# V loads issued ahead of the two stores of finished tiles, on one queue

## The reference, cut to what matters

```python
x = x + einsum('bct,bcd->bdt', x, w0[subject])        # mixes the 32 rows of a sequence
x = x + einsum('bct,bcd->bdt', x, w1[condition])
x = x + attention(x, ...)                             # below
x = x + (x @ W.T + scale * (x @ A.T) @ B.T)           # one of 8 adapters for 16 batch rows

# attention: q, k, v projected from x, rms norm and rope on q and k
k_blocks[blk, :, off] = k ; v_blocks[blk, :, off] = v # new keys and values go into the paged cache
scores = q . k_all * scale, masked to a window of 128 positions
o = softmax(scores) @ v_all ; return o @ Wo.T
```

## Time and profile before

| | |
|---|---|
| Runs | 490.85, 495.17, 505.08 us |
| Profiled execution | 493.59 us, span of the instructions 491.8 us |
| Busy share of the span | PE 78%, VectorE 70%, ScalarE 54%, GpSimd 22% |
| Mean DMA | 150 GB/s; SyncE's queue 33.5% and GpSimd's 24.9% of 16 engines' span |
| Granted TensorE clock, mean | 0.906 |
| Issue to landing, median | V write-out not told, V load 11.7 us, V rest load 8.8 us, store 7.1 us |

### The profile page before, as it was taken

The page is one execution under the profiler, slowest core; times in us unless marked ns, Lnnn a source line. Parts: engine busy times, 40 slices in busy tenths (PEclk is TensorE's granted clock), DMA queues, the critical chain, the costliest instruction groups (busy, mean ns, idle before and its releaser), DMA issues.

```text
span 491.8 us, 16903 instructions
## 1 busy us (share of the span) xinstructions
PE 381.8 (78%) x6190; PEld 283.1 (58%) x6190; DVE 345.4 (70%) x1017; ACT 264.4 (54%) x977; POOL 107.7 (22%) x178
## 2 busy tenths in 40 slices
PE   1753788888885027888798899999699999899996
PEld 0333534444442025676676777777577777777785
DVE  6995189999999515747666777777567677777782
ACT  3303556666664015646465766676456666766662
POOL 5300043333334700221112112111211212111000
PEclk9855789999998555989989999999989999999999
DMA  3999123222202266888887777967977666976200
GB/s 111 354 409 412 49 69 107 73 79 72 78 35 81 61 140 175 150 188 178 172 183 180 155 177 167 145 156 160 204 192 160 159 175 149 181 182 147 73 23 24
DMA packets 68867, 73.58 MB, mean 150 GB/s; under 512 B 18190, under 2 KB 65326, under 8 KB 66528
## 3 DMA queue, kind: packets, MB, share of 16 engines
q1 hardware_dynamic: 61968, 39.38, 33.5%
q0 software_dynamic: 6864, 33.72, 24.9%
HBM read 70.83 MB, written 26.21 MB: 197 GB/s over the span
## 4 chain that ended last, share of the span: by engine, by line
PE 48%; DMA 19%; ACT 12%; issue 11%; DVE 7%; SPq 1%; DVEq 1%; ACTq 0%; POOL 0%; POOLq 0%
ACT rope L610 6%; PE probT_bank L1128 6%; DMA kvbuf<-new_scratch,winidx 6%; PE out_bank L1152 5%; PE score_banks L1015 5%; PE score_banks L1089 5%; PE probT_bank L1015 4%; DMA value_scratch<-kvbuf 4%; PE keys_bank L1071 3%; PE score_banks L1084 3%; ACT window L601 3%; PE score_banks L1006 3%; DMA window<-value_scratch 3%; PE out_bank L1139 3%; DMA out<-early 3%
## 5 line engine op out<-in xcount | busy, mean ns | idle before, releaser
L610 ACT ACTIVATE rope<-score_banks,negm 128x176 f32<-128x176 f32 x256 | 101.8, 413 | 4.5 <-DVE negm L890 4.5
L890 DVE TENSOR_REDUCE negm<-score_banks 128x2 f32<-128x352 f32 x128 | 61.1, 519 | 34.6 <-PE score_banks L1089 34.1
L900 DVE TENSOR_SCALAR rope<-rope,rinv 128x176 f32<-128x176 f32 x256 | 70.9, 319 | 4.6
L626 ACT COPY early<-probT_bank 128x128 f32<-128x128 f32 x64 | 17.0, 266 | 88.6 <-PE probT_bank L1128 88.6
L433 POOL DMA_INDIRECT new_scratch<-stage,rowidx x32 | 36.5, 1139 | 106.7 <-DVE stage L759 101.7
L907 DVE COPY rope<-probT_bank 128x512 f32<-128x512 f32 x64 | 44.3, 692 | 18.0 <-PE probT_bank L1108 14.3
L610 ACT ACTIVATION_READ_ACCUMULATOR rope<-score_banks,negm 128x1 f32 x256 | 54.2, 212 | 0.0
L1128 PE MATMUL probT_bank<-rope,window 128*32 128x64 f32 x2048 | 43.7, 226 | 5.5 <-issue 4.7
L601 ACT COPY window<-keys_bank 128x352 f32<-128x352 f32 x60 | 46.8, 780 | 1.5 <-PE keys_bank L1071 1.5
L1071 PE MATMUL keys_bank<-ident,kvbuf 88*128 88x88 f32 x240 | 32.5, 260 | 16.3 <-ACT window L601 14.3
L1128 PEld LDWEIGHTS probT_bank<-rope,window 128*32 128x32 f32 x2048 | 32.8, 112 | 17.7 <-issue 17.7
(11 more groups left out here) (184 smaller groups left out, 734.6 us busy)
## 6 DMA issues: line engine op xcount, KB each, us to landing
value_scratch<-kvbuf SPq DMA_DIRECT2D x16, 704.0 KB
window<-value_scratch SPq DMA_DIRECT2D x16, 512.0 KB, 11.7
work<-in_x SPq DMA_DIRECT2D x16, 256.0 KB, 2.7
new_scratch<-window SPq DMA_DIRECT2D x2, 2048.0 KB, 12.1
out<-early SPq DMA_DIRECT2D x32, 128.0 KB, 7.1
window<-value_scratch SPq DMA_DIRECT2D x32, 96.0 KB, 8.8
new_scratch<-kvbuf SPq DMA_DIRECT2D x1, 2048.0 KB, 13.4
wts<-in_weights SPq DMA_DIRECT2D x1, 1280.0 KB, 8.6
```

What stands on the lines that cost most here:

```text
L610: ins = a.activation(prob[:, par, P_AT[h]:P_AT[h] + KEYS], psS[:, h, 0:KEYS], ACT.Exp, bias=negm[:, par, h:h + 1], accum_out=sums[:, par, ...
L890: v.tensor_reduce(negm[:, par, 2 * half:2 * half + 2], psS[:, 2 * half:2 * half + 2, 0:KEYS], axis=AX_X, op=ALU.max, negate=True).then_inc ...
L900: ins = v.tensor_scalar(prob[:, par, at], prob[:, par, at], rinv[:, par, h:h + 1], None, ALU.mult)
```

## The change

SyncE's calls in `step` change their order. `values_in`, with its two waits and three transfers, moves ahead of the two `store` calls, with their two waits and two transfers. Nothing else changes: no transfer, buffer, size or wait is added or removed.

```diff
             def step(grp, par):
 
                 values_out(grp, par)
+                values_in(grp, par, False)
                 if not (isinstance(grp, int) and grp == 2):
                     store(grp * 2 - 5, 1)
                 store(grp * 2 - 4, 0)
-                values_in(grp, par, False)
```

## The result

The changed kernel took 522.29 us (median of 4 runs, 519.19 to 527.18), the kernel before 495.04 (4 runs). By these medians it is slower by 27 us, 5.5%. The ratio is 1.061, 95% interval 1.053 to 1.069: all ratios here compare only executions in the faster of the two states in which a kernel is found, while the medians are over all executions (one of 916.24 us, of the changed order without gathers, is in no ratio). The prediction was 531, in a range of 500 to 560.

A forecast was written before the change was run, and what follows sets the result against it. TensorE was taken as the bound, in a tight ring with ScalarE and VectorE. Twelve steps at 3.35 us (40), plus 2 for step 2, less 6.3, gave +36 us: 531 us for the median, range 500 to 560.

The forecast's parts named there:

- V earlier is worth nothing: V loads in each step: issued 0 to 1 us earlier, with almost 8 us already to spare; taken as 0.
- The older store becomes late and stalls the copy, the newer does not matter: Stores of tiles 2g-5 and 2g-4: the first stalls ScalarE's copy 5.5 us before any relief, the second costs nothing.
- The store lands with the V loads: Older store in group 6: lands with the large V load at 302.1, while ScalarE wants its buffer at 296.57.
- the row I leaned on: Group 6 before the change: stores issued behind the 704 KB write-out landed at 289.5, its wait ending at 289.29.
- The gather ahead makes V slow, and a stall gives time back: Next group's V load: a stall shifts it S + 1.2 us from gather and write-out, so it meets less traffic.
- S = 2.15 us: ScalarE's stall per group after relief, from S = 5.5 - (S + 1.2); a group grows by 3.35 us.
- Stall plus 1.2 us: Cost of a stalled copy to its group: the stall S and 1.2 us more, from the 24.0 us stretch.
- The sum: Whole kernel: 40 us for steps 3 to 14, 2 for step 2, 0 for step 15, -6.3 replaced; +36 us.
- the late store: In the 24.0 us stretch before the change: a 13.5 us store stalled ScalarE; its 6.3 us were taken back.
- Stores landing in time: Rival: V loads run in 8 us or less, no copy stalls, -7 to +5 us, 488 to 500; chance 0.16.
- the faster outcome: Rival: long stretches and the V wait come from stores ahead of V; all 12.3 us return, 483; chance 0.04.
- No relief: Rival: a longer group does not ease traffic; ten groups cost 6.7 us each, +63, 558; chance 0.12.

## Why the prediction was right, point by point

*V earlier is worth nothing.* Shown: with four buffers the orders take the same time.

*The older store becomes late and stalls the copy, the newer does not matter.* Shown by both halves in time: 1.052 against 0.995. That the newer one never stalls its copy is wrong: with it alone behind V there were three waits of 11.4 us in sum, and in step 2 of the changed kernel one of 3.22.

*The store lands with the V loads.* Right: 0.9 us behind the large load in group 5 after, 0.7 to 0.9 in all eight steps where the older store stalled its copy, 0.4 in group 5 without rest loads. But the row I leaned on hid a second part. A quarter of the loss is the later issue as such, which I had priced at nothing: a store that meets a gather took 10.1 us with no V ahead.

*The gather ahead makes V slow, and a stall gives time back.* The first is shown by the pair without gathers. The second is seen, not isolated: stalled groups are followed by free ones. Its shape was wrong. I had every group at S = 2.15 us; in fact behind the four stalls of over 4 us the next V load took 4.5, 5.2, 5.4 and (behind that of 4.28) 7.8 us, and a stall came back a group or two later. There were nine waits in 14 steps, from 0.68 to 13.93 us, not twelve even ones.

*Stall plus 1.2 us.* This term was mis-sized. It came from one row pair. After, a wait of 13.93 us made the group 14.0 longer than 17.7, one of 6.08 made it 6.7 longer (this group took 21.5 before, with no wait), 4.79 made it 5.4, 4.28 3.7, 3.55 3.0, 2.46 only 0.9 and 1.96 only 0.5. With the usual 0.34 taken off the wait, as the prediction did, the surplus over the stall runs from 1.0 down to -1.2: short stalls are partly absorbed. The mean clock was 1.00 in the last two of these stretches and 0.78, 0.86, 0.85, 0.92 and 0.92 in the others. The clock has its price: in the stretch of 24.4 us the same 317 matmuls kept TensorE busy for 18.84 us, against 16.24 in the one of 17.6.

*The sum.* Of the 270.9 us in the middle after, 23.9 are step 2, and steps 3 to 14 hold 247.0 - 12 x 17.65 = 35 us of excess, where I had 40. Before it was 246.2, step 2 took 22.6, and 11.8 us are the excess of steps 3 to 14, of which I took back the 6.3 of the late store only. Of the other long stretches, that of 21.5 became 24.4 with a stall in it, and that of 19.1 became 17.8. 35.2 - 11.8 = 23.4, and step 2 gave 1.3, where I had 2. With the 2.0 us ahead of the first moved instruction this is the 26.7 of the profiled pair, against 36 predicted.

*Luck in it.* That 35 us came so near to 40 is in part luck. The waits of steps 3 to 14 sum to 37.8 us, where I had 12 x 2.15 = 26, and the groups grew by less than their waits, where I had 1.2 us more for each: two errors that cancel. And the longest wait, 13.93 of the 37.8, has a link that the prediction did not price, the late write-out behind a slow gather; it had V bound by TensorE's matmuls, which held in 11 of 14 steps. One reading was off and bears on nothing: from the sixteenth slice on the DMA share reads 6 to 9 tenths and then, in the last three, 2, 0 and 0, not 5 to 9.

*The rivals.* Stores landing in time is what the kernels without gathers do, and the faster outcome needed stretches that were long because of stores ahead of V; four buffers in the old order brought 1.3%, not 2.5. No relief (+63) fell: after each of the four longest stalls the V load was shorter.

*The estimate against the long landing.* By the Trainium skill, DMA: Bandwidth & Descriptors, Anatomy of one DMA, the prediction had an estimate of 3.7 us for 704 KB, and with it no stall. Without the gathers of patched blocks a V load of 512 KB alone took 4.4 us, longer than that, yet short enough that the order cost nothing; with them it took 9.4 in the median. The Trainium skill, DMA: Bandwidth & Descriptors, Issuing engines are not separate DMA queues, says that transfers of several issuing engines share the same 16 DMA engines and interleave. The trace agrees: SyncE's loads slow down with GpSimd's gather, from 4.4 to 9.4 us.

## What to carry to other kernels

When a transfer moves in a program order, ask of each transfer that it passes how soon its buffer is written again, and set its new landing (issue plus the landing of what now stands ahead) against that need; the wait that it was moved for may have had slack all along. Here the load had 8 us to spare and the store 7, and the change spent the store's. Where two buffers make the ring so tight, two more can make the order of the queue irrelevant. In this kernel that was worth more than either order.

## What the runs showed of the hardware

A store of 128 KB took 1.7 us alone, 1.8 with V loads issued behind it and no gather about, 3.4 behind V with no gather about, and 10.1 beside a gather. A large load of V took 4.2 to 4.8 us without the gathers of patched blocks on the other queue; with them it took up to 13.7 in the steps of the changed kernel, and 18.4 for group 1 ahead of them. SyncE's program itself can be held by an issue: the one at 342.33 took 5.46 us, and the second rest load of group 1, at 199.39, held it for 11.68. With the gathers gone no issue of a store took more than 0.47 us. What exactly holds an issue is not shown.
